# Node-edge count matrix of a graph kernel: 12 destinations by 10 source classes of 128 columns, one product a subtile

## The chip, the cores and the metric

The kernel runs on one core of a Trainium2 chip. The metric is the device time of one execution in microseconds (us); lower is better. The core has TensorE (matmuls, results to PSUM), VectorE, ScalarE and GpSimd, a sync engine that issues transfers, and 16 DMA engines. Each engine works through its own instructions in order, and they wait for one another by semaphores.

## The reference

Two graph layers over 1250 nodes with 512 features and 40,000 edges that are sorted by destination.

```python
h = max(layernorm(x), 0)
# layer 1: a message for each edge, summed by destination
edge_feat = concat([h[src], h[dst], edge_attr])
m = mish(mish(edge_feat @ W1 + b1) @ W2 + b2)
agg = segment_sum(m, dst)
u = mish(concat([h, agg]) @ W3 + b3)
x = x + layernorm(h + (u @ W4 + b4)) * gamma + beta
# layer 2: a weighted sum over the edges
h = max(layernorm(x), 0)
support = (h @ U * s) @ Vt
x = x + relu(segment_sum(support[src] * edge_weight[:, None], dst) + bias)
```

The second layer's sum over the edges is a product with the matrix M[destination, source], which holds the summed edge weights. M doesn't depend on the features, so the kernel builds it in the edge stage of layer 1. The change is in how M is built.

## The kernel before

Three stages follow one another: a prologue (first norm, tables of node features times W1), the edge stage, and the node stage with the second layer. The edge stage takes most of the time: it runs over 79 groups of 512 edges (the last has 64), and a group is 4 subtiles of 128 edges, j = 0 to 3. Each engine has its own program, written by hand as a sequence of steps, one for each subtile, with a loop over pairs of groups in the middle; what an engine does in step s belongs to subtiles ahead of s or behind it, by constants such as `PRE_AHEAD = 5` or `ADJ_EV_LAG = 4`.

TensorE's step is: transpose the gathered rows of subtile s + 5 (line 1125), two products that complete the first layer's input for it (lines 1133 and 1135), 12 products of 512 columns of the second layer of the message for subtile s (line 1146, `msg`), the product for M (lines 1156 and 1157, `adjacency`), and in every fourth step the sum over the destinations (line 1170, `seg`). The products run on a split of each f32 number into a high and a low part.

VectorE's step is: close mish for s + 4 (line 1321), square for s + 5 (line 1311, waits for ScalarE's exponential of line 1207, which waits for line 1135), cast the high part (line 1327), one of three preparations of a later group (lines 1287, 1290, 1294; the last in the step with j = 0), the two one-hots for M of subtile s + 1 (lines 1346 and 1347), copy the bias into the PSUM bank that the message of subtile s + 1 will use (line 1340, waited for by line 1146), close mish of the message s - 2 (line 1334), and once a group a one-hot of destinations (line 1301).

M is built like this. A source node is 8 classes (`EQ`) by 160 columns (`EC`): class = source // 160, column = source mod 160. Destinations of half a group (256 edges) lie in a window of 16 (`EWIN`); with the class they make 128 keys. For each subtile VectorE makes `so` [128 edges, 160], the one-hot of the column, and `khl` [128 edges, 2, 128], the one-hot of the key times the high and the low part of the edge weight. TensorE multiplies each of the two with `so` into the same 160 columns of the bank `pm`; the two halves of a group use two column ranges. Once a group ScalarE copies 320 columns of `pm` to `mev` (line 1242) in the step with j = 0, and GpSimd issues two transfers that add them to M in memory (line 1080). GpSimd also subtracts for the low part of hidden features (line 1061, waits for the one-hots), and issues the gathers (line 1048). The sync engine clears M at the start of the edge stage (line 371), and GpSimd waits for this before its first add.

If any half group's destinations spread wider than its window, the program takes a general path instead.

```python
i, r, half = u.const % 2, ETAIL if tail(u) else P, pm[:, u.j // HSUB * EC:(u.j // HSUB + 1) * EC]
e.matmul(half, khl[i][0:r, 0, :], so[i][0:r, :], start=u.j % HSUB == 0, stop=False, skip_group_check=True)
e.matmul(half, khl[i][0:r, 1, :], so[i][0:r, :], start=False, stop=u.j % HSUB == HSUB - 1 or tail(u), ...)
```

## Time and profile before

| | |
|---|---|
| median of 3 runs | 1515.01 us (1514.75 to 1515.66) |
| profiled execution | 1514.14 us, its span 1512.5 us |
| granted TensorE clock, mean | 0.997 of full |
| TensorE busy | 1489.6 us, 98% |
| VectorE busy | 1407.5 us, 93% |
| ScalarE busy | 1287.9 us, 85% |
| GpSimd busy | 1053.4 us, 70% |

PE is TensorE's matmul, PEld its weight load, DVE VectorE, ACT ScalarE, POOL GpSimd and SP the sync engine. Busy time is the union of the records of an engine. The records of successive instructions on one engine overlap, so what an instruction costs its engine is the distance from its start to the next one's start. An entry in square brackets at the end of a timeline row gives the idle time before it and who released it.

### The profile page before, as it was taken

Reading aid. Unit: us, or ns where it says so; the run is one execution under the profiler, and the core shown is the slowest. Engines: PE = TensorE matmul, PEld = TensorE weight load, DVE = VectorE, ACT = ScalarE, POOL = GpSimd, SP = SyncE. Lnnn points to the kernel's source line nnn. Section 1 sums busy time; section 2 is a strip of 40 time slices with the busy share of each in tenths; the row PEclk is TensorE's granted clock in tenths of the full one; section 3 lists DMA queues with packets and bytes.
Section 4 is the critical chain, followed back from the end, with each engine's and each line's share of the span. In section 5 each row is a group of like instructions: output and inputs, shape, how many; then the busy total and the mean of one; then the engine's idle time right before and its main releaser. Section 6 shows DMA issues by size and latency. Waiting matters only on the chain.

```text
span 1512.5 us, 36792 instructions
## 1 busy us (share of the span) xinstructions
PE 1489.6 (98%) x9740; PEld 1223.1 (81%) x9740; DVE 1407.5 (93%) x2841; ACT 1287.9 (85%) x2511; POOL 1053.4 (70%) x900
## 2 busy tenths in 40 slices
PE   7989999999999999999999999999999999999998
PEld 6777888888888888888888888888888888887885
DVE  7889999999999999999999999999999999996676
ACT  5088999999999999999999999999999999996562
POOL 1267778777877777877778787777877777763220
PEclk9999999999999999999999999999999999999999
DMA  8876555555554455545555554555555555544773
GB/s 293 272 218 168 122 117 115 116 124 113 114 117 119 115 113 128 114 113 117 120 115 112 123 118 115 116 121 114 112 120 121 114 115 124 112 123 100 179 165 147
DMA packets 158934, 200.26 MB, mean 132 GB/s; under 512 B 60729, under 2 KB 96569, under 8 KB 158896
## 3 DMA queue, kind: packets, MB, share of 16 engines
q0 software_dynamic: 92704, 108.04, 34.7%
q1 hardware_dynamic: 65840, 91.24, 19.5%
q10 hardware_dynamic: 352, 0.52, 0.1%
q8 instruction: 18, 0.29, 0.1%
q14 instruction: 20, 0.16, 0.0%
HBM read 151.60 MB, written 37.64 MB: 125 GB/s over the span
## 4 chain that ended last, share of the span: by engine, by line
PE 94%; DVE 2%; ACT 1%; issue 1%; DMA 1%; POOL 0%; SPq 0%; POOLq 0%; DVEq 0%; ACTq 0%
PE bm L1146 56%; PE bp L1125 7%; PE bp L1133 6%; PE bs L1170 5%; PE bp L1135 5%; PE pm L1157 2%; PE po L2123 2%; PE pu L337 2%; PE pu L2101 2%; PE pB L724 2%; PE pA L724 2%; PE pm L1156 2%; PE pu L2168 1%; DMA M_tab<-zero 1%; PE pu L2155 1%
## 5 line engine op out<-in xcount | busy, mean ns | idle before, releaser
L1061 POOL TENSOR_TENSOR hTl<-tp,hTh 128x512 fp32r<-128x512 f32 (+1 forms) x314 | 443.8, 1413 | 180.7 <-DVE khl L1347 179.8
L1146 PE MATMUL bm<-W2h,hTh 128*128 128x512 f32 x1252 | 497.5, 397 | 1.2 <-DVE bm L1340 0.8
L1146 PE MATMUL bm<-W2l,hTh 128*128 128x512 f32 x1252 | 497.5, 397 | 0.0
L1146 PE MATMUL bm<-W2h,hTl 128*128 128x512 f32 x1252 | 494.8, 395 | 0.0
L1048 POOL DMA_INDIRECT xg<-A_tab,idx x305 | 349.0, 1144 | 112.6 <-issue 63.3
L1207 ACT ACTIVATE rp<-bp 128x512 f32<-128x512 f32 (+1 forms) x314 | 186.6, 595 | 120.6 <-PE bp L1135 119.1
L1146 PEld LDWEIGHTS bm<-W2h,hTh 128*128 128x128 f32 x1252 | 235.7, 188 | 62.9 <-DVE bm L1340 6.4
L1146 PEld LDWEIGHTS bm<-W2l,hTh 128*128 128x128 f32 x1252 | 235.7, 188 | 57.4
L1146 PEld LDWEIGHTS bm<-W2h,hTl 128*128 128x128 f32 x1252 | 235.4, 188 | 56.6
L1311 DVE SCALAR_TENSOR_TENSOR rp<-rp 128x512 f32<-128x512 f32 (+1 forms) x314 | 216.6, 690 | 37.4 <-ACT rp L1207 26.0
L1321 DVE SCALAR_TENSOR_TENSOR tp<-rp,bp 128x512 f32<-128x512 f32 (+1 forms) x314 | 210.0, 669 | 4.9 <-POOL hTl L1061 2.6
L1334 DVE SCALAR_TENSOR_TENSOR tm<-rm,bm 128x512 f32<-128x512 f32 x313 | 210.1, 671 | 4.1 <-ACT rm L1235 4.1
L1340 DVE COPY bm<-b2b 128x512 f32<-128x512 f32 x309 | 210.2, 680 | 0.0
L1231 ACT ACTIVATE rm<-rm 128x512 f32<-128x512 f32 x313 | 200.1, 639 | 5.0
L1210 ACT ACTIVATE rp<-rp 128x512 f32<-128x512 f32 (+1 forms) x314 | 195.2, 622 | 6.2 <-DVE rp L1311 6.2
L1233 ACT ACTIVATE rm<-rm 128x512 f32<-128x512 f32 x313 | 195.8, 625 | 0.1
L1235 ACT ACTIVATE rm<-rm 128x512 f32<-128x512 f32 x313 | 195.5, 624 | 0.1
L1213 ACT ACTIVATE rp<-rp 128x512 f32<-128x512 f32 (+1 forms) x314 | 194.6, 620 | 0.1
L1227 ACT ACTIVATE rm<-bm 128x512 f32<-128x512 f32 x313 | 187.0, 597 | 2.3 <-DVE tm L1334 2.0
L1080 POOL DMA_DIRECT2D M_tab<-mev x157 | 165.6, 1055 | 15.5 <-issue 10.2
L1125 PE MATMUL bp<-ident_r,xg 128*128 128x128 f32 (+1 forms) x1244 | 157.2, 250 | 5.6 <-DVE tp L1321 3.7
L1347 DVE SCALAR_TENSOR_TENSOR khl<-iota_k,kcol,wcol_hl 128x256 fp32r<-128x256 f32 x313 | 147.6, 472 | 0.0
(246 smaller groups left out, 2253.3 us busy)
## 6 DMA issues: line engine op xcount, KB each, us to landing
ea<-in_eaT SPq DMA_DIRECT2D x156, 128.0 KB
M_tab<-mev POOLq DMA_DIRECT2D x157, 80.0 KB, 6.9
db<-in_dst_rows SPq DMA_DIRECT2D x78, 128.0 KB
M<-M SPq DMA_DIRECT2D x76, 128.0 KB
M_tab<-zero SPq DMA_DIRECT2D x10, 640.0 KB, 6.7
agg_tab<-ev POOLq DMA_DIRECT2D x79, 64.0 KB, 4.6
xg<-A_tab,idx POOLq DMA_INDIRECT x313
eaW<-Bh_tab SPq DMA_DIRECT2D x77, 64.0 KB
```

The source lines that it names most:

```text
L1048: e.indirect_dma_start(out=xg[p][0:r, t, :].bitcast(F32), out_offset=None, in_=A_d, in_offset=bass.IndirectOffsetOnAxis(ap=idx[p][0:r, t:t ...
L1061: e.tensor_tensor(hTl[p][:, j, 0:w], pick(u, start_t, tp)[:, 0:w], hTh[p][:, j, 0:w], ALU.subtract)\
L1125: e.matmul(bank[:, t * P:t * P + r].bitcast(F32R), xg[p][0:r, t, j * P:(j + 1) * P], ident_r[0:r, 0:r], start=t == 0, stop=False, is_trans ...
L1146: last = e.matmul(bank[0:r, :], a[p][:, c, j * P:j * P + r], w[:, c, :], start=False, stop=c == KC - 1 and w is W2l, skip_group_check=True)
L1210: e.activation(t, t, ACT.Ln, bias=1.0, scale=0.5 / (SQ * SQ)).then_inc(a_pre, 1)
L1231: e.activation(t, t, ACT.Square, bias=SQ, scale=SQ).then_inc(a_msg, 1)
L1233: e.activation(t, t, ACT.Ln, bias=0.5, scale=0.5 / (SQ * SQ)).then_inc(a_msg, 1)
L1235: e.activation(t, t, ACT.Exp, scale=-1.0).then_inc(a_msg, 1)
L1311: e.scalar_tensor_tensor(t, t, 2.0 * SQ, t, ALU.add, ALU.mult).then_inc(v_sq, 1)
L1321: e.scalar_tensor_tensor(t, pick(u, start_r, rp)[:, 0:w], 1.0, pick(u, start_bank, bp)[:, 0:w], ALU.subtract, ALU.mult).then_inc(v_pre, 2 ...
L1334: e.scalar_tensor_tensor(tm[m.const % MBUF][0:r, :], rm[m.const % 2][0:r, :], 1.0, bm[m.j][0:r, :], ALU.subtract, ALU.mult).then_inc(v_msg, 1)
L1340: e.tensor_copy(bm[m.j][:, :], b2b[:]).then_inc(v_bias, 1)
```

## The change

The classes become 10 of 128 columns, and the window 12 destinations, so that there are 120 keys. The roles of the operands are exchanged: the key's one-hot `key` [128 edges, 120] is plain, and the column's one-hot `so` [128 edges, 2, 128] carries the high and low part of the weight. One product of 256 columns a subtile puts the sums of the high parts and those of the low parts side by side in `pm`, which is now full with 2 halves x 2 parts x 128. ScalarE copies the high parts of both halves to `mev`, and a new VectorE pass, `weights`, adds the low parts from PSUM to them, once a group, in the step with j = 0 between the preparation and the one-hots. TensorE and GpSimd wait for this pass (`v_mev`) where they waited for ScalarE's copy (`a_adj`).

```diff
-EQ = 8
+EQ = 10
-EWIN = 16
+EWIN = 12
-        mev = [sb(f"mev{i}", [KEYS, 2 * EC]) for i in range(2)]
+        mev = [sb(f"mev{i}", [KEYS, 2, EC]) for i in range(2)]
-            sb1("room", [P, 80])
+            sb1("room", [P, 112])
-        so = [sb(f"so{i}", [P, EC], F32R) for i in range(2)]
-        khl = [sb(f"khl{i}", [P, 2, KEYS], F32R) for i in range(2)]
+        so = [sb(f"so{i}", [P, 2, EC], F32R) for i in range(2)]
+        key = [sb(f"key{i}", [P, KEYS], F32R) for i in range(2)]
+        v_mev = sem("v_mev")
+        def parts(n):
+            return pm[0:KEYS, 0:n * 2 * EC].rearrange("p (h a n) -> p h a n", a=2, n=EC)
 # gpsimd, adjacency
-                    e.wait_ge(a_adj, u.group(1, 1))
+                    e.wait_ge(v_mev, u.group(1, 1))
-                e.dma_start(M_d[bass.ds(b * EQ, KEYS), :], mev[u.par][:, half * EC:(half + 1) * EC], accum_op=ALU.add)\
+                e.dma_start(M_d[bass.ds(b * EQ, KEYS), :], mev[u.par][:, half, :], accum_op=ALU.add)\
 # tensor, adjacency
-                i, r, half = u.const % 2, ETAIL if tail(u) else P, pm[:, u.j // HSUB * EC:(u.j // HSUB + 1) * EC]
+                i, h, r = u.const % 2, u.j // HSUB, ETAIL if tail(u) else P
                 if u.j == 0:
-                    wait(e, a_adj, u.group())
+                    wait(e, v_mev, u.group())
                 e.wait_ge(v_adj, u.val(2, 2))
-                e.matmul(half, khl[i][0:r, 0, :], so[i][0:r, :], start=u.j % HSUB == 0, stop=False, skip_group_check=True)
-                e.matmul(half, khl[i][0:r, 1, :], so[i][0:r, :], start=False, stop=u.j % HSUB == HSUB - 1 or tail(u),
-                         skip_group_check=True).then_inc(s_adj, 1)
+                e.matmul(pm[0:KEYS, h * 2 * EC:(h + 1) * 2 * EC], key[i][0:r, :], so[i][0:r, :, :], start=u.j % HSUB == 0,
+                         stop=u.j % HSUB == HSUB - 1 or tail(u), skip_group_check=True).then_inc(s_adj, 1)
 # tensor, end of the edge stage
-            e.wait_ge(a_adj, NG)
+            e.wait_ge(v_mev, NG)
 # scalar, adjacency
-                n = EC if tail(u) else 2 * EC
-                e.activation(mev[u.par][:, 0:n], pm[:, 0:n], ACT.Copy).then_inc(a_adj, 1)
+                n = 1 if tail(u) else 2
+                e.activation(mev[u.par][:, 0:n, :], parts(n)[:, :, 0, :], ACT.Copy).then_inc(a_adj, 1)
 # vector
+            def weights(u):
+                n = 1 if tail(u) else 2
+                e.wait_ge(a_adj, u.group(1, 1))
+                e.tensor_tensor(mev[u.par][:, 0:n, :], parts(n)[:, :, 1, :], mev[u.par][:, 0:n, :], ALU.add)\
+                 .then_inc(v_mev, 1)
-                e.tensor_scalar(so[i][0:r, :], iota_q[0:r, :], scol8[0:r, c], None, ALU.is_equal).then_inc(v_adj, 1)
-                e.scalar_tensor_tensor(khl[i][0:r, :, :],
-                                       iota_k[0:r, :].rearrange("p (a k) -> p a k", a=1).to_broadcast([r, 2, KEYS]),
-                                       kcol[0:r, c],
+                e.tensor_scalar(key[i][0:r, :], iota_k[0:r, :], kcol[0:r, c], None, ALU.is_equal).then_inc(v_adj, 1)
+                e.scalar_tensor_tensor(so[i][0:r, :, :],
+                                       iota_q[0:r, :].rearrange("p (a n) -> p a n", a=1).to_broadcast([r, 2, EC]),
+                                       scol8[0:r, c],
                                        wcol_hl[0:r, c, :].rearrange("p a (h k) -> p (a h) k", k=1).bitcast(F32)
-                                       .to_broadcast([r, 2, KEYS]), ALU.is_equal, ALU.mult).then_inc(v_adj, 1)
+                                       .to_broadcast([r, 2, EC]), ALU.is_equal, ALU.mult).then_inc(v_adj, 1)
 # vector, step: behind the preparations, ahead of adjacency(s + ADJ_AHEAD)
+                g = s + -ADJ_EV_LAG
+                if g.j == 0 and g.has(MSGS):
+                    weights(g)
```

## Rows read from the trace of the kernel before

**Rows 1.** The page: busy time by engine, and the chain that ended last.

```profile
PE 1489.6 (98%) x9740; PEld 1223.1 (81%) x9740; DVE 1407.5 (93%) x2841; ACT 1287.9 (85%) x2511; POOL 1053.4 (70%) x900
...
PE 94%; DVE 2%; ACT 1%; issue 1%; DMA 1%; POOL 0%; SPq 0%; POOLq 0%; DVEq 0%; ACTq 0%
```

**Rows 2.** Busy us of each engine between 200 and 1300 us, then clock, DMA share, GB/s.

```profile
200.00:1300.00 1100.00, 1100.00 (x7422) 909.57 (x7421) 1074.24 (x2124) 1018.41 (x1993) 870.55 (x730) 1.00 0.51 117
```

**Rows 3.** Timeline of TensorE, one group: start us, duration us, engine, line, operation, tiles, shape.

```profile
703.69 0.24 PE L1156 MATMUL pm<-so,khl 128*128 128x160 f32 x1
...
716.40 0.24 PE L1156 MATMUL pm<-so,khl 128*128 128x160 f32 x1
...
716.59 0.49 PE L1125 MATMUL bp<-ident_r,xg 128*128 128x128 f32 x4
...
717.22 0.40 PE L1135 MATMUL bp<-M,eaW 128*128 128x512 f32 x1
...
720.25 0.24 PE L1156 MATMUL pm<-so,khl 128*128 128x160 f32 x1
720.32 0.27 PE L1157 MATMUL pm<-so,khl 128*128 128x160 f32 x1
720.43 0.50 PE L1125 MATMUL bp<-ident_r,xg 128*128 128x128 f32 x4
...
721.07 0.39 PE L1135 MATMUL bp<-M,eaW 128*128 128x512 f32 x1
...
721.54 0.40 PE L1146 MATMUL bm<-W2h,hTl 128*128 128x512 f32 x1
```

**Rows 4.** Timeline of VectorE in the step with j = 0.

```profile
718.28 0.69 DVE L1311 SCALAR_TENSOR_TENSOR rp<-rp 128x512 f32<-128x512 f32 x1
...
719.23 0.53 DVE L1294 TENSOR_SCALAR M<-db,base_b,iota_p 64x512 fp32r<-64x512 int32 x1
719.69 0.29 DVE L1346 TENSOR_SCALAR so<-iota_q,scol 128x160 fp32r<-128x160 f32 x1
719.90 0.47 DVE L1347 SCALAR_TENSOR_TENSOR khl<-iota_k,kcol,wcol_hl 128x256 fp32r<-128x256 f32 x1
720.29 0.68 DVE L1340 COPY bm<-b2b 128x512 f32<-128x512 f32 x1
```

**Rows 5.** Timeline of ScalarE in the same step.

```profile
717.65 0.60 ACT L1207 ACTIVATE rp<-bp 128x512 f32<-128x512 f32 x1
...
718.62 0.44 ACT L1242 ACTIVATE mev<-pm 128x320 f32<-128x320 f32 x1
```

**Rows 6.** Timeline of VectorE: two bias copies that ended late.

```profile
140.32 0.68 DVE L1340 COPY bm<-b2b 128x512 f32<-128x512 f32 x1
...
571.33 0.68 DVE L1340 COPY bm<-b2b 128x512 f32<-128x512 f32 x1
```

**Rows 7.** Timeline of TensorE: the second message matmul behind each of these.

```profile
141.39 0.40 PE L1146 MATMUL bm<-W2h,hTl 128*128 128x512 f32 x1
...
572.40 0.39 PE L1146 MATMUL bm<-W2h,hTl 128*128 128x512 f32 x1
```

**Rows 8.** Timeline of TensorE, node stage: first and last of 21 successive 256-column matmuls.

```profile
1446.02 0.27 PE L337 MATMUL pu<-nTh,W3h 128*128 128x256 f32 x1
...
1448.39 0.28 PE L337 MATMUL pu<-nTh,W3l 128*128 128x256 f32 x1
```

**Rows 9.** Timeline of TensorE: a 512-column product with transposes behind it.

```profile
71.83 0.40 PE L724 MATMUL pB<-w1l,nTh 128*128 128x512 f32 x1
72.07 0.79 PE L1125 MATMUL bp<-ident_r,xg 128*128 128x128 f32 x8
```

**Rows 10.** VectorE by line: count, busy us, mean ns, idle before; one source in PSUM.

```profile
L1938 DVE TENSOR_TENSOR aTl<-pt,aTh 128x512 fp32r<-128x512 f32 x10 | 6.4, 680 | 5.4 <-ACT aTh L1812 5.4
...
L2014 DVE TENSOR_TENSOR S<-pu,svb 128x64 f32<-128x64 f32 x8 | 1.6, 219 | 5.4 <-PE pu L2155 5.4
```

**Rows 11.** The chain that ended last, in order of time: start us, us, what.

```profile
113.19 9.55 DMA M_tab<-zero
```

## Prediction

> **What bounds the kernel now.** I read the page first. TensorE is busy for 98% of the span and carries 94% of the chain that ended last [rows 1]. That alone proves little, because a 512-column matmul has a record of 0.40 us while two of them take 0.47 us of the engine's time (721.07 to 721.54) [rows 3], so a busy TensorE can hide a wait. So I read a stretch by engine: between 200 and 1300 us TensorE shows no idle time at all, but VectorE is idle for only 25.8 us of the 1100 [rows 2]. Then I read the edge loop in order of time. Its unit is a group of four subtiles: from one line 1156 to the one four subtiles later it takes 720.25 - 703.69 = 16.56 us, and there are 78 full groups [rows 3]. Inside it TensorE starts its matmuls at even distances, so the loop goes as fast as TensorE can issue. The reader should keep two numbers of it: what lies in TensorE's row for the edited product, and how close the other engines come to holding TensorE up.
>
> The close one is VectorE's bias copy (line 1340), which fills the bank that the next subtile's msg product (line 1146) accumulates into. In the first subtile of a group (j = 0), the order is: TensorE's line 1135 at 717.22 ends at 717.62 [rows 3]; ScalarE's exponential (line 1207) runs from 717.65 to 718.25 [rows 5]; VectorE's square (line 1311), which waits for it, starts 0.03 us behind its end, at 718.28, then come the cast, line 1294 at 719.23, the one-hot at 719.69, the keys at 719.90 and the bias copy from 720.29 to 720.97 [rows 4]. TensorE starts line 1135 again at 721.07, and the second matmul behind it at 721.54 [rows 3].
>
> What happens when the copy is late is in the trace twice over. A copy that ended at 140.32 + 0.68 = 141.00 had its second matmul at 141.39, and one that ended at 571.33 + 0.68 = 572.01 had it at 572.40 [rows 6, 7]: each time 0.39 us behind the end of the copy. So the second matmul can't start before 720.97 + 0.39 = 721.36 and does start at 721.54; the spare time of VectorE at this point is 0.18 us, of which I take 0.17, as each start is rounded to 0.01.
>
> **What the change takes from TensorE.** Two products of 160 columns (lines 1156 and 1157) become one of 256. From the start of line 1156 to the next product, line 1125, is now 716.59 - 716.40 = 0.19 and 720.43 - 720.25 = 0.18 us [rows 3], mean 0.185. For 256 columns the trace has a plain stream: 20 matmuls from 1446.02 to 1448.39, so 0.118 us each [rows 8]. But here a transpose follows, and in front of a transpose the distance is longer. Behind the 160 columns of line 1157 it is 720.43 - 720.32 = 0.11 us, against 0.07 from line 1156 to 1157, and behind a 512-column product it is 72.07 - 71.83 = 0.24 [rows 9]. On the straight line between the two, 256 columns give 0.11 + 0.13 x 96/352 = 0.146 us. So TensorE saves 0.185 - 0.146 = 0.039 us a subtile; the bounds are 0.067 (0.118, nothing extra for the transpose) and 0.032 (0.118 plus the whole extra that 160 columns pay, 0.04 less rounding). In the fourth subtile of a group a different product follows (line 1170); I take the same saving. A group saves 4 x 0.039 = 0.156 us, and were nothing else in the way, 78 groups would save 12.2 us.
>
> The trace thus says 0.118 for 256 columns in a stream. The Trainium skill ("TensorE: Matmul & The Clock Gate", Back-to-back issue gap) gives columns/2.4 + 2.5 ns, that is 109 ns as an estimate, at full clock; by it a subtile would save 0.076 us, and the sum below would come out at about -6 us in place of +2.5. The trace disagrees already for plain 512-column products (0.235 us [rows 3], where the page has 216 ns).
>
> **What it puts on VectorE.** Of the two one-hots, the plain one shrinks from 160 to 120 columns and the weighted one keeps 256 elements. The plain one costs 719.90 - 719.69 = 0.21 us for 160 [rows 4]; at its share I take 0.02 off for 120 (bounds 0 and 0.05). Once a group there is a new pass, weights, 120 x 256, which adds the low sums from PSUM to what ScalarE copied. No pass like it is there, so I take it between two with the same operation and one source in PSUM: 512 elements took 680 ns, 64 took 219 ns [rows 10]. On their line 256 elements take 0.417 us; as the next instruction starts some 0.08 us ahead of a record's end (0.68 against 0.60 at line 1340), VectorE is held for 0.335. Bounds: 0.30 below, and 0.39, the distance that the weighted keys of 256 elements have now (720.29 - 719.90), above.
>
> The pass stands in the j = 0 step, between line 1294 and the one-hots, so ahead of the bias copy. This is the step with the 0.17 us of spare time. It waits for ScalarE's copy of the bank: that now runs from 718.62 to 719.06 [rows 5], and the pass could start at 719.69, 0.63 us later, so this wait costs nothing unless ScalarE slips by that much. Queued behind the pass are the two one-hots, the bias copy and tm; waiting for them are GpSimd's low part (line 1061; GpSimd is busy for 870.55 of the 1100 us [rows 2]), ScalarE's next message, and TensorE's line 1146.
>
> **The new stall.** In the j = 0 step the bias copy ends later by 0.335 - 0.02 = 0.315 us, counted from line 1135, and TensorE comes to the place 0.039 us sooner. The stall is 0.315 + 0.039 - 0.17 = 0.18 us a group. VectorE is anchored again in each group: its square waits for ScalarE, that for TensorE's line 1135 [rows 4, 5], and the segment product in the third step gives it time, so the delay neither adds up nor wears off.
>
> **Other parts.** TensorE's own new wait is in front of the product of j = 0: the bank pm must be read by weights, not only by ScalarE. The pass ends at 719.69 + 0.417 = 720.11 and the product starts at 720.25 [rows 3, 4]; the spare is thin, but what it would hold up is then missing from the stall behind it, so I count nothing. GpSimd waits for the same pass before it adds to M, two subtiles later: hidden. ScalarE's copy shrinks from 320 to 256 elements a row; no one waits on its end before 719.69, so 0. The adds to M carry 120 rows of 512 bytes for 128 of 640: nobody waits for them in the loop, 0. Zeroing M moves the same bytes in pieces of 1024 instead of 1280, 25% more of them; GpSimd waits for its end, now 9.55 us behind the last issue [rows 11], and TensorE's gather behind that. Bounds 0 and 0.25 x 9.55 = 2.4 us; the bytes are unchanged, so I take 0.4. At the end of the edge stage the last pass waits for ScalarE, while the messages on their way to TensorE have time: 0. The node stage loads the same rows of M: 0.
>
> **The sum.** A group: -0.156 + 0.18 = about +0.027 us; 78 groups: +2.1 us; with the zeroing +2.5 us. The profiled execution took 1514.14 us (a span of 1512.5 and 1.6 around it), so its like would take 1516.6. The median of the runs is 0.9 us above it, 1515.0: I predict **1517.5 us**.
>
> **Rivals.** First, faster: nothing extra is paid in front of the transpose. Then a subtile saves 0.067, the stall is 0.315 + 0.067 - 0.17 = 0.21, and a group changes by -0.268 + 0.21 = -0.058; with the zeroing -4.1 us, so 1511. The plain stream of 256 columns speaks for it, both distances in front of a transpose against it. The page's 109 ns would put it at 1509. Chance 0.17 for both. If in addition the bias copy were not what TensorE waits for, the whole saving would stand, 1502 or less; the two late copies speak against this: 0.03.
>
> Second, slower, by the same mechanism at a higher price: weights holds VectorE for 0.39 us as the other 256-element pass does. The stall grows to 0.24 us, a group to +0.08, the kernel to 1515.0 + 6.4 + 0.4 = 1522. This is slower by over 0.2% as soon as the pass holds VectorE for more than about 0.34 us. For it speaks that the keys of 256 elements do cost this; against it that they have operands, a scalar column and a broadcast, which the new pass lacks. Chance 0.26.
>
> Third, slower: VectorE becomes the bound of the whole loop. It is idle 25.8 / 1100 x 16.56 = 0.39 us a group and gets 0.335 - 4 x 0.02 = 0.26 more, so some 0.13 is left. It decides once the pass and what it collides with on GpSimd's side take over 0.4 us; at 0.6 us, the time of a full 512-element pass, the loop would be 0.29 us a group longer: 1538. Chance 0.07.
>
> That the change doesn't do what it says would need a half group whose destinations span 12 or more, which sends the kernel through its general path. The drawn destinations span at most 10 within any 256 sorted edges, so I give it nothing.
>
> **The chances.** The forecast has 0.47, and its own range, from the rounding of the distances (0.01 us a group is 0.8 us), is 1515 to 1520. With the faster rival on one side and the 0.39 us pass on the other the range is 1510 to 1523.5. A measurement of this kernel tells about 0.2%, 3 us, from no change. Faster by more: 0.19. Slower by more, from half of what lies above 1518 in the forecast's own range and both slow rivals: 0.40. Within: 0.41.
>
> **What would show it.** In the profile after: line 1156 followed by line 1125 after 0.145 us (0.118 if the first rival holds); one weights instruction a group of 0.42 us, starting where the one-hot started; the bias copy of the j = 0 step some 0.3 us later against line 1135; the second line 1146 behind it 0.39 us after the copy's end and 0.65 us after line 1135 instead of 0.47; a group of 16.59 us. The forecast is wrong if that second matmul still follows at 0.47, or if VectorE's square in the j = 0 step no longer waits for ScalarE.

## The result and the profile after

The kernel after takes 1580.2 us (1579.1 to 1584.1), the kernel before on the same chip 1515.3: a ratio of 1.0436 [1.0423, 1.0449], 65 us slower. The forecast was 1517.5 and its range ended at 1523.5; the slowest rival was 1538, with a chance of 0.07. A group of four subtiles took 16.58 us on the mean between 200 and 1300 us and takes 17.50 now.

The page of the kernel after, the rows that answer to [rows 1] (line numbers have moved: 1146 is now 1151, 1156 and 1157 are 1161, 1125 is 1130, 1207 is 1211, 1311 is 1322, 1340 is 1351, 1061 is 1066, 1048 is 1053, 1080 is 1085; `weights` is 1305):

```profile
PE 1498.6 (95%) x9427; PEld 1162.5 (74%) x9427; DVE 1490.5 (94%) x2920; ACT 1305.6 (83%) x2511; POOL 1158.6 (73%) x900
...
issue 34%; POOL 31%; PE 16%; POOLq 8%; DVE 6%; ACT 2%; DMA 2%; SPq 0%; DVEq 0%; ACTq 0%
```

TensorE carried 94% of the chain; now GpSimd (POOL) and issue carry it. The busy time from 200 to 1300 us, as in [rows 2], shows that TensorE has idle time (49.65 us) and VectorE less than before (11.9 for 25.8):

```profile
200.00:1300.00 1100.00, 1050.35 (x6791) 811.62 (x6784) 1088.06 (x2077) 980.91 (x1889) 917.00 (x693) 1.00 0.47 108
```

So I went by line (count, busy us, mean ns, idle before; 200 to 1300 us). VectorE's square took 691 ns on the mean before, GpSimd's gather 1142:

```profile
L1322 DVE SCALAR_TENSOR_TENSOR rp<-rp 128x512 f32<-128x512 f32 x251 | 238.8, 951 | 11.8 <-ACT rp L1211 11.8
...
L1066 POOL TENSOR_TENSOR hTl<-tp,hTh 128x512 fp32r<-128x512 f32 x252 | 385.5, 1530 | 141.5 <-DVE so L1358 141.5
L1053 POOL DMA_INDIRECT xg<-A_tab,idx x252 | 381.0, 1512 | 41.0 <-issue 32.2
```

The 0.26 us of the mean isn't spread: 61 of the 251 squares, one a group, take 1.8 us (one more takes 1.2) and the others 0.68. A long square costs VectorE 1.1 us, and the group grew by 0.92 us only, as the change saves TensorE time elsewhere (below). VectorE's timeline around one of them (start us, us, engine, line):

```profile
698.84 0.41 DVE L1305 TENSOR_TENSOR mev<-pm,mev 120x256 f32<-120x256 f32 x1
699.18 0.26 DVE L1357 TENSOR_SCALAR key<-iota_k,kcol 128x120 fp32r<-128x120 f32 x1
699.37 0.47 DVE L1358 SCALAR_TENSOR_TENSOR so<-iota_q,scol,wcol_hl 128x256 fp32r<-128x256 f32 x1
699.76 0.68 DVE L1351 COPY bm<-b2b 128x512 f32<-128x512 f32 x1
...
701.55 0.67 DVE L1322 SCALAR_TENSOR_TENSOR rp<-rp 128x512 f32<-128x512 f32 x1
702.15 0.41 DVE L1338 CAST hTh<-tp 128x512 fp32r<-128x512 f32 x1
...
703.07 0.68 DVE L1351 COPY bm<-b2b 128x512 f32<-128x512 f32 x1
703.67 0.67 DVE L1345 SCALAR_TENSOR_TENSOR tm<-rm,bm 128x512 f32<-128x512 f32 x1
704.26 0.67 DVE L1332 SCALAR_TENSOR_TENSOR tp<-rp,bp 128x512 f32<-128x512 f32 x1
705.12 1.80 DVE L1322 SCALAR_TENSOR_TENSOR rp<-rp 128x512 f32<-128x512 f32 x1 [0.19 <-ACT rp L1211]
```

And GpSimd's:

```profile
699.91 1.30 POOL L1066 TENSOR_TENSOR hTl<-tp,hTh 128x512 fp32r<-128x512 f32 x1 [1.69 <-DVE so L1358]
701.35 2.65 POOL L1053 DMA_INDIRECT xg<-A_tab,idx  x1
703.98 1.04 POOL L1085 DMA_DIRECT2D M_tab<-mev  x1
704.61 1.76 POOL L1066 TENSOR_TENSOR hTl<-tp,hTh 128x512 fp32r<-128x512 f32 x1
```

Read from the end. The square starts at 705.12, while GpSimd's subtraction runs (704.61 to 706.37), and ends 0.55 us after it. The subtraction is late because the gather of the j = 0 step took 2.65 us; the same gather took 0.98 us in the kernel before. In this stretch 62 of 63 gathers of that step take 2.65 us and one 2.06. TensorE then waits for the bias copy behind the square (the row is of the group before):

```profile
696.31 0.50 PE L1151 MATMUL bm<-W2h,hTh 128*128 128x512 f32 x1 [0.78 <-DVE bm L1351]
```

The first theory that I tested, A: GpSimd and VectorE shut each other out, and the place of their instructions in time decides how much it costs. Its rivals: B, VectorE simply has too much work; C, the exchanged operands are to blame. The Trainium skill ("SBUF — State Buffer", Who interferes with whom) states a rule of that kind: a VectorE instruction with two SBUF inputs contends with a GpSimd instruction that reads SBUF, and one in a two-port mode contends with GpSimd in general; the one that was issued first has the shared ports for its whole length and the other waits. Copies, casts and compares with a scalar can be in such a mode. The long square (its two inputs are one SBUF tile, GpSimd's subtraction reads SBUF and was issued first) fits this, and its record agrees: 1.80 us for 0.68, with the end 0.55 us behind the subtraction's.

### The profile page after: what moved, and what is told of

Its sections match the earlier page's. It is cut to its first block, busy times and chain, and to the rows that moved or that the text cites. A ratio compares the mean times of both kernels' runs of the same rounds, so it can differ in the third digit from the quotient of the medians.

```text
span 1577.8 us, 36280 instructions
## 1 busy us (share of the span) xinstructions
PE 1498.6 (95%) x9427; PEld 1162.5 (74%) x9427; DVE 1490.5 (94%) x2920; ACT 1305.6 (83%) x2511; POOL 1158.6 (73%) x900
## 4 chain that ended last, share of the span: by engine, by line
issue 34%; POOL 31%; PE 16%; POOLq 8%; DVE 6%; ACT 2%; DMA 2%; SPq 0%; DVEq 0%; ACTq 0%
POOL xg L1053 13%; POOL hTl L1066 9%; POOL M_tab L1085 6%; PE bm L1151 4%; POOLq L1079 4%; POOL agg_tab L1074 3%; POOLq L1071 2%; PE po L2137 2%; PE pu L337 2%; PE pu L2115 2%; PE pA L724 1%; PE pB L724 1%; PE pu L2182 1%; DVE bm L1351 1%; DVE so L1358 1%
## 5 line engine op out<-in xcount | busy, mean ns | idle before, releaser
L1066 POOL TENSOR_TENSOR hTl<-tp,hTh 128x512 fp32r<-128x512 f32 (+1 forms) x314 | 472.4, 1505 | 188.1 <-DVE so L1358 187.2
L1151 PE MATMUL bm<-W2h,hTh 128*128 128x512 f32 x1252 | 511.5, 409 | 54.9 <-DVE bm L1351 54.7
L1053 POOL DMA_INDIRECT xg<-A_tab,idx x305 | 455.3, 1493 | 68.3 <-issue 39.2
L1151 PE MATMUL bm<-W2l,hTh 128*128 128x512 f32 x1252 | 491.4, 392 | 0.0
L1322 DVE SCALAR_TENSOR_TENSOR rp<-rp 128x512 f32<-128x512 f32 (+1 forms) x314 | 291.3, 928 | 20.6 <-ACT rp L1211 20.5
L1085 POOL DMA_DIRECT2D M_tab<-mev x157 | 161.1, 1026 | 14.7 <-issue 10.1
L1130 PE MATMUL bp<-ident_r,xg 128*128 128x128 f32 (+1 forms) x1244 | 149.6, 244 | 5.2 <-DVE tp L1332 3.1
L1130 PEld LDWEIGHTS bp<-ident_r,xg 128*128 128x128 f32 (+1 forms) x1244 | 130.1, 140 | 29.6 <-issue 17.7
```

What stands on the lines that cost most here:

```text
L1053: e.indirect_dma_start(out=xg[p][0:r, t, :].bitcast(F32), out_offset=None, in_=A_d, in_offset=bass.IndirectOffsetOnAxis(ap=idx[p][0:r, t:t ...
L1066: e.tensor_tensor(hTl[p][:, j, 0:w], pick(u, start_t, tp)[:, 0:w], hTh[p][:, j, 0:w], ALU.subtract)\
L1085: e.dma_start(M_d[bass.ds(b * EQ, KEYS), :], mev[u.par][:, half, :], accum_op=ALU.add)\
L1130: e.matmul(bank[:, t * P:t * P + r].bitcast(F32R), xg[p][0:r, t, j * P:(j + 1) * P], ident_r[0:r, 0:r], start=t == 0, stop=False, is_trans ...
L1151: last = e.matmul(bank[0:r, :], a[p][:, c, j * P:j * P + r], w[:, c, :], start=False, stop=c == KC - 1 and w is W2l, skip_group_check=True)
L1322: e.scalar_tensor_tensor(t, t, 2.0 * SQ, t, ALU.add, ALU.mult).then_inc(v_sq, 1)
```

## The experiments

**Is it the pass?** In e1 the pass is left out (so M lacks the low parts of the weights), in e2 it is put alone into the kernel before, with its waits and an unused result.

```diff
# e1, kernel after
-                if g.j == 0 and g.has(MSGS):
-                    weights(g)
# and v_mev -> a_adj in the three waits
# e2, kernel before
+                if g.j == 0 and g.has(MSGS):
+                    weights(g)   # tensor_tensor of 256 elements, pm + b2b -> unused tile, then_inc(v_mev)
```

> The changed kernel with the pass weights left out; the low sums are therefore missing from M, and TensorE and GpSimd wait for ScalarE's copy as before. Theory A (a lost race for an SBUF port: the pass shifts GpSimd's gather against VectorE's cast, the gather of the j = 0 step then takes 2.65 us, GpSimd's next subtraction runs late and holds VectorE's square for 1.2 us once a group): the square keeps 0.68 us, the gather 1.0 us, and the loop runs at TensorE's pace with 0.067 us saved a subtile, 1494 to 1500 us. Theory B (VectorE is simply overloaded, in proportion to the work added): about the same here, 1494 to 1500. Theory C (the exchanged operands or the full PSUM bank cost the time, not the pass): stays above 1560.

> The kernel before with one thing added: a VectorE addition of 128 x 256 from pm in the j = 0 step, where weights stands in the changed kernel, with TensorE and GpSimd waiting for it; its result goes to a spare tile that nobody reads, M is computed as before. Theory A: gather of 2.65 us and a square of 1.8 us once a group, so 1580 to 1595 us. Theory B: about 20 us over the kernel before (0.34 us a group, less the idle 0.39). Theory C: within 1515 to 1535.

e1: 1514.4 us, 0.9996 [0.9981, 1.001], above the 1494 to 1500 that A and B both expected. Groups of 16.0, 16.6 and 17.2 us are mixed; 52 gathers still take 2.0 us or more, and 51 squares 1.2 or 1.8 us. So the pass isn't needed for the collision, but without it many groups escape. e2: 1528.4 us, 1.0094 [1.0077, 1.011], a group 0.17 us longer and no long gather or square; A in its first form had expected 1580 to 1595 and B about 1535; the time lies in C's range (1515 to 1535), and C falls only with e4 and e17 below. The pass alone costs what the prediction's stall says when TensorE saves nothing and the one-hots are the old ones (0.335 - 0.17 = 0.165 us). e2 shows one thing more: its gathers of the j = 0 step have the distances of the long ones in the kernel after (square 0.18 to 0.20 us behind the gather's start, cast 0.78 to 0.80) and all take 0.98 us. So the distance to VectorE's next instructions alone doesn't decide.

**Is it GpSimd's place in time?** In e4 GpSimd's subtraction of the j = 0 step waits for the key's one-hot and not for both. The subtraction reads neither of them; it only uses their count as a clock. e7 is the same in the kernel without the pass (M again without low parts), e6 the same in the kernel before.

```diff
-                    e.wait_ge(v_adj, u.val(2, 2 * (ADJ_AHEAD - DVE_PRE + 1)))
+                    e.wait_ge(v_adj, u.val(2, 2 * (ADJ_AHEAD - DVE_PRE + 1) - (1 if u.j == 0 else 0)))
```

> The changed kernel, but GpSimd's subtraction of the j = 0 step waits for the plain one-hot (key) instead of for the weighted one (so) behind it. Theory A: subtraction and gather start up to 0.15 us earlier against VectorE, the gather gets the port ahead of the cast: 1512 to 1525 us. If the subtraction starts ahead of the weighted one-hot it may hold that up by 1 us and the kernel stays near 1580. Theory B and C: 1580.

> The pass weights left out (M lacks the low sums), and GpSimd's subtraction of the j = 0 step waits for the plain one-hot. Theory A: no collision; what remains is TensorE's saving of 0.067 us a subtile, 1515 - 21 = 1494, at most 1499. The difference to the changed kernel with the same early subtraction (1505.1) is then the price of the pass alone, 0.1 to 0.15 us a group. Theory B: as without the early subtraction, 1514.

> The kernel before, with one wait changed: in the step with j = 0 GpSimd's subtraction waits for the first of VectorE's two one-hots (line 1346) and not for both, so it and the gather behind it start some 0.2 us earlier. The same edit on the kernel after gave 1505.1 us in place of 1576. Collision theory (the edit only takes away the long gather and the long square that follow in the kernel after): the kernel before has neither, TensorE never waits, so 1513 to 1516.5 us and a group of 16.55 to 16.60 us. Theory that an earlier subtraction is a gain of its own (VectorE or TensorE waits for GpSimd in the kernel before as well): 1503 to 1509 us.

e4: 1505.1 us, 0.9937 [0.9921, 0.9954]: 75 us less by one wait of GpSimd that starts it earlier, and below the kernel before. GpSimd's timeline, then VectorE's square of the same step:

```profile
699.07 1.47 POOL L1066 TENSOR_TENSOR hTl<-tp,hTh 128x512 fp32r<-128x512 f32 x1 [1.30 <-DVE key L1357]
700.69 0.98 POOL L1053 DMA_INDIRECT xg<-A_tab,idx  x1
701.65 1.04 POOL L1085 DMA_DIRECT2D M_tab<-mev  x1
```

```profile
701.10 0.67 DVE L1322 SCALAR_TENSOR_TENSOR rp<-rp 128x512 f32<-128x512 f32 x1
```

The gather is back at 0.98 us, and no square is long. The square starts 0.41 us behind the gather's start here, 0.20 in the kernel after. e7: 1482.7 us, 0.9787 [0.9771, 0.9804], below the 1494 expected; the pass costs 1505.1 - 1482.7 = 22 us, 0.29 us for each of the 78 groups. e6: 1514.4 us, 0.9997 [0.9988, 1.0007]: in the kernel before there is nothing to win by it. B and C as causes of the 65 us fall here: e4 has the same work and operands as the kernel after.

**What holds the gather?** Six variants of the kernel after, each with one thing moved. e3: a memset of one column behind the square at j = 1; e5: a reduction of 128 elements there; e11: that reduction ahead of the square; e12: the register load for the transfer behind the gather moved ahead of the subtraction; e13: the transfer itself moved there; e8: the transfers at other steps.

```diff
# e5 (e3: a memset of 1 column; e11: the same two lines ahead of square(v))
+                if s.reg is not None and s.const % 4 == 1:
+                    e.tensor_reduce(tick[:, 0:1], b2b[:, 0:128], AX.X, ALU.max)
# e13 (e12: only the value_load), ahead of low(s + DVE_PRE)
+                if s.j == 0 and (s + -8).has(4 * FULL):
+                    adjacency(s + -8, 1)
# e8
-    ADJ_LAG = {2: (6, 0), 0: (8, 1)}
+    ADJ_LAG = {3: (7, 0), 1: (9, 1)}
```

> The changed kernel with one more VectorE instruction: a memset of one column between the square and the cast of the j = 1 step in the loop, some 0.06 to 0.1 us. Theory A: the cast comes that much later, the gather gets the port first, and the kernel becomes faster although VectorE has more to do: 1512 to 1525 us, no square of 1.8 us. Theory B and C: 1580 to 1590, slower by the memset.

> The changed kernel with VectorE's cast of the j = 1 step held back by a reduction of 128 elements in front of it (0.1 to 0.2 us; the one-column memset tried before moved the cast by 0.01 us only). Theory A (the cast beats GpSimd's gather to an SBUF port by some 0.01 us, and the late subtraction then blocks the square): the cast comes 0.9 us or more behind the gather's start instead of 0.80, the gather takes 1.0 us, no square takes 1.8 us, and with 0.15 us more to do on VectorE the kernel is faster, 1505 to 1525 us. Theory B (VectorE overloaded in proportion to its work): 1585 to 1595 us.

> The kernel after, with a reduction of 128 elements (0.2 us or more of VectorE) put ahead of the square in every step with j = 1; the same reduction behind the square gave 1595.9 us, with gathers of 2.8 us. It moves the start of the square from 0.19 us behind the gather's start to about 0.4 us. Theory that the square's start within some 0.2 us of the gather's start keeps GpSimd from reading: the gather takes 1.0 to 1.1 us, the subtraction behind it runs off the square, no square of 1.8 us remains, and although VectorE has more work the kernel gets faster: 1510 to 1545 us, a group of 16.5 to 16.9 us. Theory that VectorE as a whole is too full, or that the gather is held by whatever VectorE runs: 1590 to 1600 us again, a group of 17.7 us, gathers of 2.6 us or more.

> The kernel after, with one register load of GpSimd moved: the row number for the second transfer into M (line 1081 of the kernel after), which was read from SBUF directly behind the gather of the j = 0 step, is read ahead of the subtraction of that step, where GpSimd waits anyway. The instructions with a record stay in their order. Theory that the register load is what VectorE's two-port work keeps out, and that the gather's record of 2.65 us contains its wait (the long gathers occur only where a transfer into M follows the gather: j = 0 in the kernel after, j = 3 where the transfers were moved to j = 3 and 1): gathers of 1.0 to 1.1 us in all steps, no square of 1.8 us, a group of 16.35 to 16.65 us, 1500 to 1518 us. Theory that the gather itself is kept out by the square that starts 0.19 us behind it: nothing changes, 1572 to 1584 us, gathers of 2.65 us.

> The kernel after, with the second transfer into M (the half-1 call of GpSimd's adjacency) issued ahead of the subtraction of the j = 0 step, where GpSimd otherwise waits some 1.7 us for VectorE's one-hot, in place of behind that step's gather. Subtraction and gather keep their starts; what follows the gather is now the next subtraction. Theory that only a gather with a transfer directly behind it is drawn out (long ones were at j = 0 in the kernel after and at j = 3 where the transfers stood there): gathers of 1.0 to 1.1 us in the j = 0 step though the square starts 0.19 us behind them, no square of 1.8 us, a group of 16.4 to 16.5 us, 1500 to 1512 us. Theory that the gather is drawn out by what VectorE runs alone, whatever GpSimd does next: gathers of 2.65 us remain, the subtraction starts 0.6 us earlier for the missing transfer, and the square of the next step still meets some of it: 1525 to 1560 us.

> The changed kernel, but GpSimd issues its two adds to M in the steps with j = 3 and j = 1 instead of j = 2 and j = 0, so that none stands between the long gather and the next subtraction. It tests the second link of theory A: the gather still loses the port (2.65 us), but the subtraction starts about 0.6 us sooner and overlaps the square by 0.2 to 0.5 us instead of 1.1; the square takes 0.8 to 1.3 us, and the kernel 1530 to 1555 us. If the long gather itself cost the time, and not the blocked square: 1580.

| run | us | ratio | long gathers of the j = 0 step | squares |
|---|---|---|---|---|
| e3 | 1576.4 | 1.0409 [1.0391, 1.0426] | 7 of 2.1 us, 56 of 2.65 us | 7 of 1.2 us, 56 of 1.8 us |
| e5 | 1595.9 | 1.0537 [1.052, 1.0555] | 2.85 us | 2.0 us |
| e11 | 1568.0 | 1.035 [1.0333, 1.0367] | 2.45 us | 1.6 us |
| e12 | 1579.5 | 1.0415 [1.0398, 1.0433] | 2.65 us | 1.8 us |
| e13 | 1513.4 | 0.9994 [0.9985, 1.0003] | 2.7 us | 0.7 to 0.8 us |
| e8 | 1554.3 | 1.0259 [1.0241, 1.0276] | 9 of 2.7 us; some 50 of 2.1 us at j = 3 | 9 of 1.3 us |

e3 moved the cast by 0.01 us only and tests nothing. The others refute what each was made for: not the cast's distance (e5), not the square's (e11), not the register load (e12), not the transfer behind it (e13). But e13 shows the second half of the chain by itself. The gather is as long as ever, and the run is 67 us faster than the kernel after, because the subtraction behind it now starts early enough to miss most of the square. The long gather itself costs little; the late subtraction costs VectorE 1.1 us a group.

One thing is common to the long gathers: in the kernel after, e3, e5, e12 and e17 (below) nearly all end 0.3 us behind the start of `tm` (VectorE's line 1345; 701.35 + 2.65 = 704.00 against 703.67), so just behind the end of the bias copy; in e1 41 of 52 end 0.3 us behind the start of the bias copy. In e5 VectorE's row is 0.2 us longer by the reduction, and so is the gather (2.85 for 2.65). The VectorE instructions in that time keep their length (0.41 and 0.68 us). This fits a GpSimd that waits through the unbroken row from the cast to the one-hot or the bias copy. No run isolates that wait: in short gathers the cast next to it is often drawn out instead (0.44 for 0.41 us), in e2 and in e17 the same row stands beside short gathers too, and e11 (end 0.5 us behind the bias copy's start) fits less well.

**GpSimd adds in place of VectorE.** ScalarE copies all 512 columns to a tile, GpSimd adds the halves.

```diff
+                    e.tensor_tensor(mev[u.par][:, 0:n, :], raw[:, 0:n, 0, :], raw[:, 0:n, 1, :], ALU.add).then_inc(g_mev, 1)
-                e.activation(mev[u.par][:, 0:n, :], parts(n)[:, :, 0, :], ACT.Copy).then_inc(a_adj, 1)
+                e.activation(raw[:, 0:n, :, :], parts(n), ACT.Copy).then_inc(a_adj, 1)
```

> The sum of high and low parts taken off VectorE: ScalarE copies all 512 columns of the bank to a tile of its own, and GpSimd adds the two parts there, in the step of its first add to M; the reference's M is complete. Theory A: without VectorE's pass the collision depends on where VectorE stands to GpSimd, as in the kernel without the pass (1514): between 1497 and 1520, with gathers of 2.65 us in a part of the groups; GpSimd's new addition of two SBUF tiles may block a square or a one-hot itself, 0.5 us a group. Theory B: 1496 to 1500, as VectorE has less to do than before.

1547.8 us, 1.0219 [1.0202, 1.0236], above what both theories expected. Only 5 gathers take over 2 us, but 42 squares take 1.1 us, 10 squares 1.6 to 1.8, and 65 casts some 1.0 us (0.41 where nothing meets them). VectorE has no pass here and still loses to GpSimd's extra work.

**Does it need the change at all?** The kernel before, with e11's reduction (e14), and with a memset of 128 columns on GpSimd between subtraction and gather of the j = 0 step as well (e17).

```diff
+                    if s.reg is not None and s.const % 4 == 1:
+                        e.tensor_reduce(tick[:, 0:1], b2b[:, 0:128], AX.X, ALU.max)
                     square(v)
# e17, gpsimd, ahead of the gather
+                if s.j == 0 and s.reg is not None:
+                    e.memset(gtick[:, :], 0.0)
```

> The kernel before, with nothing of the change but a reduction of 128 elements (0.2 us of VectorE) put ahead of the square in every step with j = 1, so that VectorE has an instruction starting 0.2 us behind the gather's start, where it waits some 0.1 us for ScalarE in the kernel before. VectorE is idle for 0.39 us a group and takes 0.2 us of it. Theory that the long gather comes from VectorE's leaving no gap at the gather's start, in the kernel before as in the kernel after: gathers of 2.4 us and squares of 1.5 to 1.8 us appear once a group, a group of 17.2 to 17.4 us, 1565 to 1582 us. Theory that the changed operands, or the pass itself, are needed for it: gathers of 1.0 to 1.1 us, a group of 16.55 to 16.65 us, 1514 to 1520 us.

> The kernel before with the reduction of 128 elements ahead of VectorE's square in the steps with j = 1, as in the run without effect (1515.3 us), and with a memset of 128 columns on GpSimd between subtraction and gather of the j = 0 step, so that the gather starts some 0.3 us later; no part of the change. It puts ScalarE's message square at 0.3 to 0.5 us behind the gather's start (0.65 to 0.75 us in the run without the memset) and VectorE's square at 0.05 to 0.15 us. Theory that the place in time of the three engines to one another is the whole cause: in the groups where ScalarE's square lies under 0.44 us the gather takes 2 us or more and VectorE's square of the next step 1.2 to 1.8 us, and the group grows from 16.57 to over 16.9 us, 1530 to 1580 us, if the memset takes 0.3 us. Theory that something of the change (its operands, its sizes) is needed: gathers of 1.0 to 1.1 us wherever they start, 1514 to 1520 us.

e14: 1515.3 us, 1.0 [0.9991, 1.0009], no long gather; to fill VectorE's gap isn't enough. e17: 1568.8 us (two executions), 1.0357 [1.0336, 1.0377]. This is the kernel before with 0.2 us of extra work a group on VectorE and a gather that starts 0.15 us later (1.60 us behind the subtraction's start, for 1.45), and it has the whole pattern: nothing of the change is needed for it. GpSimd's gather, two groups of the same run:

```profile
325.97 0.98 POOL L1050 DMA_INDIRECT xg<-A_tab,idx  x1
...
342.81 2.71 POOL L1050 DMA_INDIRECT xg<-A_tab,idx  x1 [0.16 <-issue]
```

VectorE beside them:

```profile
326.20 0.67 DVE L1315 SCALAR_TENSOR_TENSOR rp<-rp 128x512 f32<-128x512 f32 x1
326.80 0.41 DVE L1331 CAST hTh<-tp 128x512 fp32r<-128x512 f32 x1
...
343.04 0.67 DVE L1315 SCALAR_TENSOR_TENSOR rp<-rp 128x512 f32<-128x512 f32 x1
343.64 0.41 DVE L1331 CAST hTh<-tp 128x512 fp32r<-128x512 f32 x1
...
345.18 0.66 DVE L1338 SCALAR_TENSOR_TENSOR tm<-rm,bm 128x512 f32<-128x512 f32 x1
...
346.57 1.90 DVE L1315 SCALAR_TENSOR_TENSOR rp<-rp 128x512 f32<-128x512 f32 x1
```

Both times the square starts 0.23 us behind the gather, with the same instructions behind it. The first eight groups from 200 us are short (16.57 us), then from 342 us on all 55 are long (17.49). So the loop has two paces and stays in the long one once it has fallen into it. That the long square makes VectorE late and so brings the next gather into the same trouble is likely, but not shown step by step.

**What tips it over?** The trace of the kernel before has a small disturbance of its own. Once in seven groups GpSimd issues its transfer of the segment sums (line 1069) some 0.4 us late; the subtraction behind it comes later, and VectorE's one-hot (line 1301) takes 1.3 to 1.4 us for 1.0:

```profile
330.05 1.19 POOL L1069 DMA_DIRECT2D agg_tab<-ev  x1 [0.38 <-issue]
```

There it costs 0.04 to 0.16 us once, and the next group is normal again. e17 has the same late transfer, and the long one-hot behind it:

```profile
331.91 1.19 POOL L1071 DMA_DIRECT2D agg_tab<-ev  x1 [0.36 <-issue]
```

```profile
333.27 1.31 DVE L1305 TENSOR_TENSOR oh<-iota_w,drel 128x128 f32<-128x128 f32 x1
```

VectorE and GpSimd are then some 0.25 us later against TensorE and ScalarE than in the groups before, and the next gather of the j = 0 step, at 342.81, is the first long one. In e15 (below), and in e1 near 330 us, the change of pace also follows such a transfer. Why GpSimd is late there, no run tells.

**Is ScalarE part of it?** Over the runs, short and long gathers of the j = 0 step at the same distance to the square differed by ScalarE's message square: 0.36 to 0.43 us behind the gather's start for the long, 0.44 and more for the short. A copy between exponential and square at j = 1 moves it, 64 columns in e16 and 320 in e18:

```diff
+                    if not pre and k == 0 and s.reg is not None and s.const % 4 == 1:
+                        e.activation(tick[:, :], bm[m.j][:, 0:320], ACT.Copy)
```

> The kernel after, with a copy of 64 columns on ScalarE (0.15 to 0.25 us) put between the message's exponential and its square (line 1235) in every step with j = 1; nothing on VectorE or GpSimd is changed. In all runs so far the gathers of the j = 0 step fall apart by one number: where ScalarE's message square starts 0.33 to 0.44 us behind the gather's start, and VectorE has no gap, the gather takes 2.06 to 2.85 us; where it starts 0.45 us behind or later the gather takes 0.98 to 1.06 us. Theory that ScalarE's place in time is the cause: its square now starts about 0.6 us behind the gather, gathers of 1.0 us, no square of 1.8 us on VectorE, a group of 16.4 to 16.6 us, 1500 to 1518 us. Theory that the two only go together, and VectorE's row of instructions alone holds the gather: gathers of 2.65 us, 1572 to 1590 us.

> The kernel after, with a ScalarE copy of 320 columns from the message's PSUM bank put between the message's exponential and its square in every step with j = 1. The copy of 64 columns in the run before this one cost ScalarE nothing: it lay in the 0.6 us between the two, and the square moved by 0.01 us, so that run tested nothing. This one moves the square to 0.6 us or more behind the gather's start, where ScalarE stands in all gathers that stayed short (0.45 us and later), and until then ScalarE reads PSUM, as there. Theory that ScalarE's place in time decides whether the gather gets through: gathers of 1.0 us, a group of 16.4 to 16.6 us, 1500 to 1520 us. Theory that ScalarE's place is only a mark of which engine the others wait for, and doesn't act on the gather: gathers of 2.65 us, 1575 to 1595 us.

e16 (1578.7 us, 1.0428 [1.0411, 1.0446]) moved the square by 0.01 us, since the copy lay in ScalarE's own wait. e18 moved it to 0.59 us behind a gather at 212.83:

```profile
213.42 0.63 ACT L1236 ACTIVATE rm<-rm 128x512 f32<-128x512 f32 x1
```

and takes 1579.4 us, 1.0426 [1.041, 1.0442], with 63 long gathers. The place of this square is a mark of the long pace, not its cause. ScalarE's exponential and TensorE's products were not moved, so their place against the gather is not tested.

**What bounds the loop without the collision?** e15 is e4 with VectorE's preparation of 0.46 us (line 1298) moved from the j = 0 step, where it stood ahead of the pass, to j = 1; e19 moves it to j = 2 and lets the subtraction of j = 2 go early too.

```diff
-    PREP_AHEAD = (9, 8, 6)
+    PREP_AHEAD = (9, 6, 6)     # e15: (9, 7, 6)
-                    e.wait_ge(v_adj, u.val(2, 2 * (ADJ_AHEAD - DVE_PRE + 1)))
+                    e.wait_ge(v_adj, u.val(2, 2 * (ADJ_AHEAD - DVE_PRE + 1) - (1 if u.j in (0, 2) else 0)))
```

> The kernel after with GpSimd's early subtraction (1505.1 us, a group of 16.42 us), and also VectorE's third preparation (0.46 us) moved from the step with j = 0 to the one with j = 1 (PREP_AHEAD 9, 7, 6), so that the j = 0 step holds the pass without it. Theory that the group of 16.42 us is set by the late bias copy of the j = 0 step (the stall of the prediction): the stall goes, and the group falls to what TensorE issues, 16.1 to 16.2 us, 1482 to 1490 us. Theory that VectorE's whole work of a group is the bound there (16.57 - 0.39 idle + 0.335 pass - 0.08 keys = 16.43 us): no gain, 1502 to 1508 us. If the moved preparation fills VectorE's gap at the gather of the j = 0 step, long gathers come back: over 1550 us.

> The kernel after, with GpSimd's early subtraction in the steps with j = 0 and j = 2, and VectorE's third preparation (0.46 us) moved from the step with j = 0 to the one with j = 2 (PREP_AHEAD 9, 6, 6). With the preparation in the step with j = 1 the groups ran 16.1 to 16.2 us for a while, until the gather of that step was held and the kernel fell to 17.1 us a group. Theory that the stall in the j = 0 step makes the 16.42 us of the kernel with the early subtraction alone, and that its removal lasts if no gather starts 0.0 to 0.2 us ahead of VectorE's square: a group of 16.1 to 16.3 us, 1480 to 1497 us, faster than both kernels. Theory that VectorE's whole work bounds the group: 1502 to 1508 us. If a gather or a one-hot meets GpSimd in its new place: over 1525 us.

e15: 1539.8 us, 1.018 [1.0157, 1.0203]. It is two runs in one: busy time from 200 to 330 us and from 340 us on,

```profile
200.00:330.00 130.00, 130.00 (x869) 105.12 (x869) 127.44 (x265) 121.38 (x242) 102.81 (x89) 1.00 0.51 117
340.00:1300.00 960.00, 919.16 (x6083) 729.70 (x6086) 960.00 (x1857) 860.60 (x1689) 806.87 (x618) 1.00 0.48 111
```

with groups of 16.1 to 16.2 us and no idle TensorE, then groups of 17.1 us, from the first long gather (341.29, at j = 1) on. e19: **1474.1 us, 0.9737 [0.9723, 0.975]**, groups of 16.0 us, no long square or gather. It beats both kernels, with all of the change in it. The two moves of e19 were not tried on the kernel before (e6 is only the wait of j = 0), so how much of the 2.6% is the change's own isn't shown.

## Why the prediction was wrong, step by step

**TensorE's saving: right in kind, too small.** From the product for M to the transpose it takes 0.12 us, the first rival's 0.118 and not the 0.146 that I took. From e19, TensorE:

```profile
699.28 0.39 PE L1151 MATMUL bm<-W2h,hTl 128*128 128x512 f32 x1
...
701.54 0.40 PE L1151 MATMUL bm<-W2l,hTh 128*128 128x512 f32 x1
701.78 0.28 PE L1161 MATMUL pm<-so,key 128*120 128x256 f32 x1
701.90 0.46 PE L1130 MATMUL bp<-ident_r,xg 128*128 128x128 f32 x4
702.19 0.47 PE L1138 MATMUL bp<-M,eaW 128*128 128x512 f32 x1
```

The line through 160 and 512 columns was the wrong tool: what is extra in front of a transpose didn't grow with the columns here (0.12 against 0.118 for 256). The saving is 3 x (0.185 - 0.12) + 0.074 in front of the segment product = 0.27 us a group, for 0.156. Two more terms I did not have at all. The message products follow one another after 0.2297 us on the mean in e19 and after 0.2337 in the kernel before (the ten distances from 699.28 to 701.54 are 0.226 each): 48 times 0.004, and 0.02 in front of the product, is 0.21 us. From the transposes to the next product it is 0.313 for 0.338, four times 0.025 = 0.10. Together 0.58 us, and e19's group is 15.99 for 16.57. The shorter distances between message products (medians of 0.227 to 0.229 us for 0.232) stand in every kernel with the new product and in none with the old ones; why, no run tells.

**The pass: right.** It holds VectorE from 698.84 to 699.18, 0.34 for the 0.335, with a record of 0.41. The second rival's 0.39 fell.

**The stall: right.** In the kernel after, TensorE in a step with j = 0:

```profile
699.38 0.38 PE L1161 MATMUL pm<-so,key 128*120 128x256 f32 x1
...
700.19 0.40 PE L1140 MATMUL bp<-M,eaW 128*128 128x512 f32 x1
700.49 0.50 PE L1151 MATMUL bm<-W2h,hTh 128*128 128x512 f32 x1
700.83 0.39 PE L1151 MATMUL bm<-W2h,hTl 128*128 128x512 f32 x1
```

The second message product starts 0.39 us behind the end of the bias copy (699.76 + 0.68 = 700.44) and 0.64 us behind line 1140, where the forecast had 0.39 and 0.65. The wait in front of the product for M, which the prediction counted as nothing, is real: the product starts at 699.38, 0.13 us behind the end of the pass and 0.42 us behind the last message product, for 0.23 without the pass. But the second message product still waits for the bias copy, so this wait adds nothing to the stall, as argued. e2 shows the stall alone (0.17 for 0.165). With the real saving of 0.58 / 4 = 0.145 us a step the prediction's formula gives 0.315 + 0.145 - 0.17 = 0.29 us, and e4 against e7 gives 0.29.

In part this last agreement is luck, for e7 mixes two paces: groups in which VectorE's one-hot of line 1312 takes 0.4 us last 15.99 us, as in e19, and those in which it takes 1.0 us last 16.17. In e4 it takes 1.07 us on the mean; like against like the stall is 16.43 - 16.17 = 0.26 us, and 0.18 of what e19 gains over e4 (16.43 to 15.99) goes with the short one-hot. VectorE is idle for 0.19 us a group in e4 and 0.23 in e19, so its work as a whole, the core of the third rival, isn't what TensorE waits for in either.

**The zeroing** (0.4 us in the sum): the row of [rows 11] reads 8.60 us in the kernel after and 10.96 in e19, for 9.55. No run separates this term.

**What failed: "queued behind the pass ... GpSimd's low part".** I named who waits for the delayed one-hots and gave it no price, because GpSimd was idle for a fifth of the time [rows 2]. The share was the wrong view. What counts is where GpSimd's instructions lie beside VectorE's. In the kernel before, the subtraction behind that gather ended 0.57 us ahead of VectorE's next square (708.86 and 709.43). There it started 2.23 us behind the gather's start (705.34 to 707.57); in the kernel after it starts 3.26 us behind it (701.35 to 704.61), because the gather was held for 1.67 us, and the square that it then meets loses 1.1 us. "The delay neither adds up nor wears off" failed with it: once a gather is held, nearly every one behind it is (62 of 63 groups). The third rival named a collision on GpSimd's side, with a chance of 0.07 and 0.29 us a group; the loop got 0.92 us longer. Its 0.29 us doesn't come from VectorE's idle time either, which would give 0.6 - 0.08 - 0.39 = 0.13; it is the stall formula with a pass of 0.6 us. I had a price for VectorE's extra work but none for a collision, although the trace of before has the same kind once a group: its one-hot of line 1301 took 1.03 us, and without a collision in e19 (line 1312) 0.34.

```profile
L1301 DVE TENSOR_TENSOR oh<-iota_w,drel 128x128 f32<-128x128 f32 x66 | 68.3, 1035 | 0.0
```

```profile
L1312 DVE TENSOR_TENSOR oh<-iota_w,drel 128x128 f32<-128x128 f32 x68 | 23.4, 344 | 0.0
```

**Open:** why at the same distances to VectorE (0.23 us in e17) the gather is short in one group and long in the next, beyond that a late transfer comes between them; what GpSimd waits for inside the gather; and why the message products got closer.

## What to carry to other kernels

When a change shifts VectorE by some tenths of a microsecond, lay its timeline beside GpSimd's and list each pair that comes to overlap, with the length that such a pair has where the trace already shows one; busy shares don't show this. A wait that only serves as a clock (here the subtraction's on the one-hots) is a dial: turn it before giving up a change, since the same change cost 4.4% in one place in time and, with two waits and one preparation moved, gained 2.6% in another. And price a saving on the bound engine from each of its distances, not only those of the edited product.

## What the runs showed of the hardware

- The loop has two stable paces (16.57 and 17.49 us a group in e17, 16.1 and 17.1 in e15); the long one was entered in the middle of one execution, behind a transfer that GpSimd issued 0.4 us late (0.6 in e15), and not left again by 1300 us. e1 and e7, without the pass, change between their paces several times.
- A gather's issue on GpSimd took 2.65 us for 0.98 beside a row of VectorE instructions that start 0.2 to 0.6 us apart, and ended close behind that row. The rule of the Trainium skill ("SBUF — State Buffer", Who interferes with whom) speaks of one instruction's length; here it was three to five in a row. That the row holds the gather is read from where the ends lie, and beside the same row other gathers took 0.98 us (e2).
- GpSimd's subtraction and VectorE's square together took VectorE 1.80 us for 0.68; the one-hot with two SBUF inputs took 1.03 us beside GpSimd's work and 0.34 without.
- A ScalarE copy of 64 columns (record 0.25 us) and a VectorE memset of one column moved the instructions behind them by 0.01 us.
